# Row statistics of a layer norm: from one engine's statistics instruction to another's two accumulating passes

## The chip, the cores and the metric

The kernel runs on one core of a Trainium2 chip. The metric is the time on the device in microseconds (us), lower is better. Three runs of the kernel before took 1511.75, 1512.75 and 1513.91 us, so its median is 1512.75 us. The engines of a core: TensorE (PE in the profile; PEld are its weight loads), VectorE (DVE), ScalarE (ACT), GpSimd (POOL) and SyncE (SP), which here only issues DMAs. Each engine works through its own instructions in order and waits on semaphores for the others.

## The reference, cut to what matters

```python
def reference(x, adj, W_q, b_q, W_k, b_k, W_v, b_v):     # x: 4096 x 512, adj: 4096 x 4096 of 0 and 1
    m = mean(x, axis=-1); v = var(x, axis=-1)
    h = maximum((x - m) / sqrt(v + 1e-5), 0)             # layer norm of every row, then relu
    q, k, v = h @ W_q.T + b_q, h @ W_k.T + b_k, h @ W_v.T + b_v
    z = (q @ k.T) / sqrt(512) * adj
    z = where(z == 0, -10000.0, z)
    return x + relu(softmax(z, axis=1) @ v)
```

All inputs and the output are float32. The change concerns the first two lines alone.

## The kernel before, in words

The 4096 rows of x are cut into 32 tiles of 128 rows, and these into 8 quads of 4 tiles (QUAD, QUADS). The kernel has two parts.

The **opening** makes everything that the attention needs: the normalised rows h, their halves of 16 bits (a high and a low part, so that float16 products give nearly float32), V = h Wv, and G, the product of h with M = Wk Wq (project_g), in the form of seven operands of a Strassen-like product. It is a loop over k in 0 .. 40 that every engine walks in its own order: slot k = 4g + i, with i = 0 .. 3. In the text "slot i" means this i, and four slots make a period. In slot k:

- TensorE (lines 627 to 643): the first or third piece of the scores of one pair of tiles (`scores(begun, 0)` where i is odd, `scores(ended, 2)` where it is even), the V tile k (`project_v`, L475), the second or fourth piece of the scores, the transpose of h tile k + 4 (`transpose_h`, L457), and a part of G of the quad before (`project_g`, L489). Scores of pairs are made in the opening from slot 9 on. All products of the scores stand at L502.
- ScalarE (lines 836 to 875): `copy_m1` (L747) and `copy_m2` of the pair begun, or `copy_u4` and `copy_d` of the pair ended; `high_v(k)` (L705); `copy_u2`, `copy_m7` or `copy_c12`; `high_g` (L724) where i is 0 or 2; `high_h(k+4)` (L697); in slot i = 2 the root of the quad g + 2 (`square_root`, L681); `normalise(k+5)` (L688); and `copy_g` (L713). TensorE's next piece of the scores waits for the first copy of the pair (m1 or u4), because it accumulates into the same bank.
- VectorE (lines 1245 to 1303): `add_c2`, then in slot 3 `quad_rstd` (reciprocal of the root, one Newton step, and the shift, from L972 to L982), `combine_g`, `low_v` (L1009), `low_g` (L1029), `low_h` (L1003), `add_c11`, `weigh` (times the adjacency, L1101), `row_dot` (L990), `negate`, `see_min` (the running minimum, L1117), and in slot i = 1 the statistics of quad g + 2: four `row_stats` (L954), four `aggregate` (L960) and `quad_var` (L965 and L966).

The normalisation of a quad goes around the engines so: mean and variance on VectorE, `var_eps` (variance + epsilon), root on ScalarE, `quad_rstd` on VectorE, then `normalise` on ScalarE with scale and bias per row, one tile per slot. A quad of x is loaded by SP (`load_x`, L310) into one of two buffers, o_rows or p_buf, once the quad before in that buffer has been normalised: quads 0 and 1 at the start, quad 2 after the first, and `load_x(g + 3)` in period g.

The **main part** (L502 and L558 in turn) then goes over 8 blocks of 512 query rows with 16 pairs of key tiles each: scores, exponential, and the sum over V. It has no part in the change. Ahead of the opening's loop stands a start (lines 1197 to 1243 on VectorE, 821 to 834 on ScalarE) in which the quads 0 and 1 and the weights are prepared; there the statistics of quad 1 stand between `largest_m(1)` and `row_dot(2)`, and its aggregates after `low_h(3)`.

Of the kernel before, what the change touches and what calls it, by code (L numbers as in the profile page):

```python
# [13 lines left out]
P = 128  # L14
NODES = 4096
DIM = 512
# [32 lines left out]
def adj_preln_attention(nc, x, adj_t, wq, bq, wk, bk, wv_t, bv, out, g_dram, v_dram, h_dram):  # L49
# [15 lines left out]
    with ctx:  # L65
        def sb(name, shape, dt):
            return ctx.enter_context(nc.sbuf_tensor(name, shape, dt))
# [41 lines left out]
        b_cols = sb("b_cols", [P, 2, KC], F32)  # L109
        stats = sb("stats", [P, QUAD, 6], F32)  # L110
        mean_var = sb("mean_var", [P, QUAD, 2], F32)
        mean = sb("mean", [P, TILES], F32)
        var_eps = sb("var_eps", [P, TILES], F32)
        root = sb("root", [P, TILES], F32)
        rstd = sb("rstd", [P, TILES], F32)
# [79 lines left out]
        m_lo_ready = sem("m_lo_ready")  # L195
        stats_ready = sem("stats_ready")
        aggregated = sem("aggregated")
        var_ready = sem("var_ready")
        root_ready = sem("root_ready")
        newton_seq = sem("newton_seq")  # L200
# [476 lines left out]
        def _(act):  # L677
            def square_root(q):
                act.wait_ge(var_ready, q + 1)
                span = slice(q * QUAD, (q + 1) * QUAD)  # L680
                nc.scalar.activation(root[:, span], var_eps[:, span], ACT.Sqrt).then_inc(root_ready, 1)  # L681

            def normalise(t):
                act.wait_ge(rstd_ready, t // QUAD + 1)
                if t >= 2:
                    act.wait_ge(hT_ready, t - 1)
                    act.wait_ge(dots_done, t - 1)
                nc.scalar.activation(normal[t % 2], x_quad[t // QUAD % 2][:, t % QUAD, :], ACT.Relu,  # L688
                                     bias=shift[:, t:t + 1], scale=rstd[:, t:t + 1]).then_inc(normed, 1)
# [131 lines left out]
            square_root(0)  # L821
            normalise(0)
            normalise(1)
            act.wait_ge(wv_loaded, 16)
            for k in range(KC):
                high_wv(k)
# [1 line left out]
            high_h(1)  # L828
            normalise(2)
            normalise(3)  # L830
            high_h(2)
            high_h(3)
            square_root(1)
# [2 lines left out]
            for k in range(PARTS):  # L836
                g, i = k // QUAD, k % QUAD
                begun, ended = opening_pair(k), opening_pair(k - 1)
                if begun >= 0:
                    copy_m1(begun)  # L840
                    copy_m2(begun)
                if ended >= 0:
                    copy_u4(ended)
                    copy_d(ended)
                if k == 1:
                    high_m(0)
                    high_m(1)
                if k == 2:
                    high_m(2)
                    high_m(3)  # L850
                if g < QUADS:
                    high_v(k)
                if begun >= 0:
                    copy_u2(begun)
                    copy_m7(begun)
                if ended >= 0:
                    copy_c12(ended)
                if i == 2 and 1 <= g <= QUADS:
                    high_g(g - 1, 0)
                if i == 0 and 2 <= g <= QUADS + 1:  # L860
                    high_g(g - 2, 1)
                if g + 1 < QUADS:
                    high_h(k + QUAD)
                if k in (5, 6):
                    high_t(0, 2 * (k - 5))
                    high_t(0, 2 * (k - 5) + 1)
                if k in (36, 37):
                    high_t(1, 2 * (k - 36))
                    high_t(1, 2 * (k - 36) + 1)
                if i == 2 and g + 2 < QUADS:  # L870
                    square_root(g + 2)
                if k + QUAD + 1 < TILES:
                    normalise(k + QUAD + 1)
                if 1 <= g <= QUADS:
                    copy_g(g - 1, i)

            for n in range(-3, STEPS):
                s, j = n // PAIRS, n % PAIRS
# [47 lines left out]
        def _(dve):  # L926
# [19 lines left out]
                dve.wait_ge(scales_ready, k + 1)  # L946

            def row_stats(t):
                q = t // QUAD
                if t % QUAD == 0:  # L950
                    dve.wait_ge(x_loaded[q % 2], 16 * (q // 2 + 1))
                    if q > 0:
                        dve.wait_ge(aggregated, QUAD * q)
                v.bn_stats(stats[:, t % QUAD, :], x_quad[q % 2][:, t % QUAD, :]).then_inc(stats_ready, 1)  # L954

            def aggregate(t):
                dve.wait_ge(stats_ready, t + 1)
                if t % QUAD == 0 and t > 0:
                    dve.wait_ge(var_ready, t // QUAD)
                v.bn_aggr(mean_var[:, t % QUAD, :], stats[:, t % QUAD, :]).then_inc(aggregated, 1)  # L960

            def quad_var(q):
                span = slice(q * QUAD, (q + 1) * QUAD)
                dve.wait_ge(aggregated, QUAD * q + QUAD)
                v.tensor_copy(mean[:, span], mean_var[:, :, 0])  # L965
                v.tensor_scalar(var_eps[:, span], mean_var[:, :, 1], EPS, None, ALU.add).then_inc(var_ready, 1)  # L966

            def quad_rstd(q):
                span = slice(q * QUAD, (q + 1) * QUAD)
                r = rstd[:, span]  # L970
                dve.wait_ge(root_ready, q + 1)
                v.reciprocal(r, root[:, span]).then_inc(newton_seq, 1)  # L972
                dve.wait_ge(newton_seq, 4 * q + 1)
                v.tensor_tensor(newton[:, :], r, r, ALU.mult).then_inc(newton_seq, 1)
                dve.wait_ge(newton_seq, 4 * q + 2)
                v.scalar_tensor_tensor(out=newton[:, :], in0=newton[:, :], scalar=-0.5, in1=var_eps[:, span],
                                       op0=ALU.mult, op1=ALU.mult).then_inc(newton_seq, 1)
                dve.wait_ge(newton_seq, 4 * q + 3)
                v.scalar_tensor_tensor(out=r, in0=newton[:, :], scalar=1.5, in1=r,
                                       op0=ALU.add, op1=ALU.mult).then_inc(newton_seq, 1)  # L980
                dve.wait_ge(newton_seq, 4 * q + 4)
                v.scalar_tensor_tensor(out=shift[:, span], in0=mean[:, span], scalar=-1.0, in1=r,  # L982
                                       op0=ALU.mult, op1=ALU.mult).then_inc(rstd_ready, 1)

            def row_dot(t):
                dve.wait_ge(normed, t + 1)
# [216 lines left out]
                row_stats(t)  # L1203
            for t in range(QUAD):
                aggregate(t)
            quad_var(0)
            dve.wait_ge(u_row_ready, 1)
            v.tensor_copy(u_row, u_row_bank).then_inc(u_row_copied, 1)
            quad_rstd(0)
# [18 lines left out]
            link(largest(mag[1][:, KC:KC + 1], u_cols[:, :]))  # L1228
            link(v.tensor_scalar(mag[1][:, KC:KC + 1], mag[1][:, KC:KC + 1], 1.0 / DIM, None, ALU.mult))
            largest_m(1)  # L1230
            for t in range(QUAD, 2 * QUAD):
                row_stats(t)
            row_dot(2)
            low_h(2)
            row_dot(3)
            low_h(3)
            for t in range(QUAD, 2 * QUAD):
                aggregate(t)
            quad_var(1)
            key_terms(0)  # L1240
            largest_m(2)
            quad_rstd(1)
            largest_m(3).then_inc(mag_ready, 1)

            for k in range(PARTS + 2):
# [47 lines left out]
                if k in (37, 38):  # L1293
                    low_t(1, 2 * (k - 37))
                    low_t(1, 2 * (k - 37) + 1)
                if i == 1 and g + 2 < QUADS:
                    for t in range(QUAD):
                        row_stats(QUAD * (g + 2) + t)
                    for t in range(QUAD):
                        aggregate(QUAD * (g + 2) + t)  # L1300
                    quad_var(g + 2)
                if i == 3 and g + 1 < QUADS:
                    key_terms(g + 1)
# [98 lines left out]
```

## Time and profile before

| | |
|---|---|
| median of 3 runs | 1512.75 us |
| the profiled execution's own time | 1509.94 us |
| its span, first to last instruction | 1508.2 us |
| mean granted TensorE clock | 0.998 |
| TensorE busy | 1478.0 us, 98% of the span |
| VectorE busy | 1272.7 us, 84% |
| ScalarE busy | 878.8 us, 58% |
| GpSimd busy | 1.7 us |
| DMA | 304.92 MB, mean 202 GB/s |

The opening lasts from about 37 to 305 us of the span. How to read the profile: "line engine operation out<-in" is a group of instructions, with starts and durations in us from the span's start. Behind one another, operations of an engine overlap a little, so the distance from start to start is shorter than the duration. In square brackets stands for how long the engine was idle before, and what released it. The granted clock is a share of TensorE's full 2.4 GHz.

### The profile page before, as it was taken

The numbers are of one execution on the slowest core, as the hardware profiler recorded it, in microseconds if no ns is written. First come the engines' busy times: TensorE is split into PE (matmuls) and PEld (weight loads), VectorE is DVE, ScalarE is ACT, GpSimd is POOL, SyncE is SP. The second block draws the span as 40 slices with busy tenths as digits, with TensorE's granted clock in tenths as the row PEclk, the third lists the DMA queues.
The fourth block names the chain that finished last, engine by engine and source line by source line (L and its number), as shares of the span: only waits on it lengthen the run. The fifth ranks groups of instructions, "written<-read, shape, count | busy, mean of one in ns | idle before, by whom it ended". The sixth has DMA issues, their size and how long they took to land.

```text
span 1508.2 us, 24869 instructions
## 1 busy us (share of the span) xinstructions
PE 1478.0 (98%) x9550; PEld 941.3 (62%) x9550; DVE 1272.7 (84%) x1570; ACT 878.8 (58%) x1402; POOL 1.7 (0%) x11
## 2 busy tenths in 40 slices
PE   8899999889999999999999999999999999999998
PEld 4456665566666666666666666666666666666544
DVE  6878887898898889798988898889978897988875
ACT  2566665575566556665656555655665566555542
POOL 0000000000000000000000000000000000000000
PEclk9999999999999999999999999999999999999999
DMA  5255544485555655566646665566556655655252
GB/s 202 98 183 203 201 161 161 159 300 205 222 207 194 249 211 220 210 225 229 222 194 238 238 231 196 207 236 238 209 212 223 226 210 209 217 212 191 86 168 84
DMA packets 75478, 304.92 MB, mean 202 GB/s; under 512 B 8416, under 2 KB 8416, under 8 KB 73568
## 3 DMA queue, kind: packets, MB, share of 16 engines
q1 hardware_dynamic: 75360, 303.33, 54.6%
q8 instruction: 76, 1.25, 0.3%
q14 instruction: 42, 0.34, 0.1%
HBM read 264.51 MB, written 38.80 MB: 201 GB/s over the span
## 4 chain that ended last, share of the span: by engine, by line
PE 92%; DVE 4%; issue 2%; ACT 1%; DMA 1%; SPq 0%; DVEq 0%; POOLq 0%; POOL 0%; ACTq 0%
PE o L558 44%; PE za L502 22%; PE zd L502 11%; PE zb L502 5%; PE o L475 5%; PE o L489 4%; DMA o_rows<-in_x 1%; PE o L457 1%; DVE stats L954 0%; PE za L586 0%; DVE run_min L1117 0%; ACT g_buf L724 0%; PE za L578 0%; PE za L570 0%; DVE o_rows L1172 0%
## 5 line engine op out<-in xcount | busy, mean ns | idle before, releaser
L558 PE MATMUL o<-v_buf,p_buf 128*128 128x512 f16 x3072 | 734.8, 379 | 3.3 <-issue 3.3
L558 PEld LDWEIGHTS o<-v_buf,p_buf 128*128 128x128 f16 x3072 | 300.5, 98 | 272.0 <-issue 3.5
L502 PE MATMUL za<-h_buf,g_buf 128*128 128x256 f16 x2976 | 405.8, 273 | 7.6 <-ACT mm_tmp L747 3.4
L502 PEld LDWEIGHTS za<-h_buf,g_buf 128*128 128x128 f16 x2976 | 289.6, 98 | 144.8 <-ACT mm_tmp L747 5.3
L502 PE MATMUL zd<-h_buf,g_buf 128*128 128x256 f16 x1488 | 203.0, 273 | 0.0
L1093 DVE TENSOR_TENSOR slots<-um_tmp,dm_tmp 128x512 f32<-128x512 f32 x128 | 88.4, 690 | 108.8 <-ACT dm_tmp L774 108.7
L1140 DVE TENSOR_TENSOR p_buf<-slots,p_buf 128x1024 f16<-128x1024 f32 x128 | 156.1, 1219 | 21.7 <-PE o L558 20.1
L786 ACT ACTIVATE slots<-slots,log_p 128x1024 f32<-128x1024 f32 x128 | 145.9, 1140 | 37.3 <-DVE slots L1133 37.3
L781 ACT ACTIVATE slots<-za,c_all,kappa 128x256 f32<-128x256 f32 x128 | 72.3, 565 | 145.5 <-PE za L502 144.7
L1105 DVE SCALAR_TENSOR_TENSOR slots<-slots 128x1024 f32<-128x1024 f32 x128 | 156.0, 1219 | 0.2
L1133 DVE TENSOR_TENSOR slots<-slots,floor_b 128x1024 f32<-128x1024 f32 x128 | 155.8, 1218 | 0.4 <-ACT floor_b L799 0.4
L502 PEld LDWEIGHTS zd<-h_buf,g_buf 128*128 128x128 f16 x1488 | 145.6, 98 | 16.9
L747 ACT ACTIVATE mm_tmp<-za,c_all,kappa 128x256 f32<-128x256 f32 x128 | 72.4, 566 | 139.8 <-PE za L502 135.8
L1151 DVE TENSOR_TENSOR acc<-acc,slots 128x1024 f32<-128x1024 f32 x112 | 136.5, 1219 | 0.5
L1117 DVE TENSOR_TENSOR run_min<-run_min,slots 128x1024 f32<-128x1024 f32 x112 | 136.4, 1218 | 0.0
L793 ACT CAST p_buf<-slots 128x1024 f16<-128x1024 f32 x128 | 132.9, 1038 | 3.7 <-PE o L558 3.2
L1101 DVE TENSOR_TENSOR slots<-slots,adj_own 128x1024 f32<-128x1024 f32 x91 | 111.4, 1224 | 15.0 <-ACT slots L781 7.7
L759 ACT ACTIVATE um_tmp<-za,c_all,kappa 128x256 f32<-128x256 f32 x128 | 72.4, 566 | 70.8 <-PE za L502 62.7
L502 PE MATMUL zb<-h_buf,g_buf 128*128 128x256 f16 x744 | 101.5, 273 | 0.0
L769 ACT ACTIVATE um_tmp<-za,c_all,kappa 128x256 f32<-128x256 f32 x128 | 72.4, 566 | 47.9 <-PE za L502 47.2
L502 PEld LDWEIGHTS zb<-h_buf,g_buf 128*128 128x128 f16 x744 | 72.8, 98 | 8.4
L475 PE MATMUL o<-slots,h_buf 128*128 128x512 f16 x288 | 68.6, 389 | 4.7 <-DVE v_buf L1009 4.7
(151 smaller groups left out, 1104.7 us busy)
## 6 DMA issues: line engine op xcount, KB each, us to landing
g_buf<-g_dram SPq DMA_DIRECT2D x112, 896.0 KB, 5.4
v_buf<-v_dram SPq DMA_DIRECT2D x128, 512.0 KB, 3.4
adj_own<-in_adj SPq DMA_DIRECT2D x91, 512.0 KB, 6.2
spare<-in_adj SPq DMA_DIRECT2D x37, 512.0 KB, 6.2
g_dram<-g_buf SPq DMA_DIRECT2D x12, 896.0 KB, 4.5
v_dram<-v_buf SPq DMA_DIRECT2D x16, 512.0 KB, 5.3
spare<-in_x SPq DMA_DIRECT2D x15, 512.0 KB, 8.7
h_buf<-h_dram SPq DMA_DIRECT2D x7, 1024.0 KB, 9.1
```

The lines of the kernel that those rows point to most:

```text
L475: mm = pe.matmul(v_bank(t)[:, :], h[:, a, k, span], wv_pair[:, b, k, :], start=(k == 0 and m == 0), stop=(k == KC - 1 and m == 2))
L502: mm = pe.matmul(bank[:, 0:QH], g_of(i)[:, a, op, j, :], right[b][j], start=(fresh and j == 0 and m == 0), stop=(j == 1 and m == 2), skip_ ...
L558: mm = pe.matmul(o_bank[t][:, :], a[:, kt, span], v_buf[:, n % V_BUFS, kt, b, :], start=(j == 0 and kt == 0 and m == 0), stop=(j == PAIRS ...
L786: nc.scalar.activation(slot(n), slot(n), ACT.Exp, bias=log_p[:, 0:1], scale=-UNIT).then_inc(p_ready, 1)
L793: nc.scalar.copy(p_hi[n % 3], slot(n)).then_inc(p_hi_ready, 1)
L1093: v.tensor_tensor(slot(i)[:, 1, :], um_tmp[:, :, :].rearrange("p a n -> p (a n)"), dm_tmp[:, :, :].rearrange("p a n -> p (a n)"), ALU.add) ...
L1101: v.tensor_tensor(slot(i), slot(i), adj_buf[adj_slot(i)], ALU.mult).then_inc(weighted, 1)
L1105: v.scalar_tensor_tensor(out=slot(i), in0=slot(i), scalar=0.0, in1=slot(i), op0=ALU.is_equal, op1=ALU.subtract).then_inc(negated, 1)
L1117: v.tensor_tensor(run_min[:, :, :], run_min[:, :, :], slot(i), ALU.min).then_inc(min_seen, 1)
L1133: v.tensor_tensor(slot(n), slot(n), floor_b[:, :].unsqueeze(1).to_broadcast([P, 2, QW]), ALU.subtract).then_inc(lowered, 1)
L1140: v.tensor_tensor(p_lo[n % 2], slot(n), p_hi[n % 3], ALU.subtract).then_inc(p_lo_ready, 1)
L1151: v.tensor_tensor(acc[:, :, :], acc[:, :, :], slot(n), ALU.add).then_inc(summed, 1)
```

## The change

For quad 0 nothing changes but the sign that is kept with the mean. From quad 1 on the four `bn_stats`, four `bn_aggr` and the copy of the mean on VectorE are gone. In their place ScalarE goes twice over every tile of x: `row_mean` computes -x/512 into a float16 tile that nobody reads and sums it along the row into `neg_mean`, and `row_squares` computes (x + neg_mean) squared into the same tile and sums it into `squares`. `quad_var` on VectorE becomes one small operation, squares/512 + epsilon. In the loop the four mean passes of quad g + 2 stand at the end of ScalarE's slot i = 0, its four passes of squares at the end of slot i = 1, and `quad_var` at the end of VectorE's slot i = 2. `square_root` stays in the middle of ScalarE's slot i = 2.

```diff
+        neg_mean = sb("neg_mean", [P, TILES], F32)
+        squares = sb("squares", [P, TILES], F32)
+        sum_waste = sb("sum_waste", [P, 2, DIM], F16)
...
+            def row_mean(t):
+                q = t // QUAD
+                if t % QUAD == 0:
+                    act.wait_ge(x_loaded[q % 2], 16 * (q // 2 + 1))
+                    if q >= 2:
+                        act.wait_ge(squares_ready, t - QUAD)
+                elif t % QUAD >= 2:
+                    act.wait_ge(means_ready, t - QUAD - 1)
+                nc.scalar.activation(sum_waste[:, t % 2, :], x_quad[q % 2][:, t % QUAD, :], ACT.Copy, scale=-1.0 / DIM,
+                                     accum_out=neg_mean[:, t:t + 1]).then_inc(means_ready, 1)
+
+            def row_squares(t):
+                act.wait_ge(means_ready, t // QUAD * QUAD)
+                if t % QUAD >= 2:
+                    act.wait_ge(squares_ready, t - QUAD - 1)
+                nc.scalar.activation(sum_waste[:, t % 2, :], x_quad[t // QUAD % 2][:, t % QUAD, :], ACT.Square,
+                                     bias=neg_mean[:, t:t + 1], accum_out=squares[:, t:t + 1]
+                                     ).then_inc(squares_ready, 1)
...
             square_root(0)
             normalise(0)
             normalise(1)
+            for t in range(QUAD, 2 * QUAD):
+                row_mean(t)
             act.wait_ge(wv_loaded, 16)
...
             normalise(2)
             normalise(3)
+            for t in range(QUAD, 2 * QUAD):
+                row_squares(t)
             high_h(2)
...
                 if 1 <= g <= QUADS:
                     copy_g(g - 1, i)
+                if g + 2 < QUADS:
+                    for t in range(QUAD):
+                        if i == 0:
+                            row_mean(QUAD * (g + 2) + t)
+                        if i == 1:
+                            row_squares(QUAD * (g + 2) + t)
...
             def quad_var(q):
                 span = slice(q * QUAD, (q + 1) * QUAD)
-                dve.wait_ge(aggregated, QUAD * q + QUAD)
-                v.tensor_copy(mean[:, span], mean_var[:, :, 0])
-                v.tensor_scalar(var_eps[:, span], mean_var[:, :, 1], EPS, None, ALU.add).then_inc(var_ready, 1)
+                dve.wait_ge(squares_ready, QUAD * (q - 1) + QUAD)
+                v.tensor_scalar(var_eps[:, span], squares[:, span], 1.0 / DIM, EPS, ALU.mult, ALU.add
+                                ).then_inc(var_ready, 1)
...
-                v.scalar_tensor_tensor(out=shift[:, span], in0=mean[:, span], scalar=-1.0, in1=r,
-                                       op0=ALU.mult, op1=ALU.mult).then_inc(rstd_ready, 1)
+                v.tensor_tensor(shift[:, span], neg_mean[:, span], r, ALU.mult).then_inc(rstd_ready, 1)
...
             largest_m(1)
-            for t in range(QUAD, 2 * QUAD):
-                row_stats(t)
             row_dot(2)
             low_h(2)
             row_dot(3)
             low_h(3)
-            for t in range(QUAD, 2 * QUAD):
-                aggregate(t)
-            quad_var(1)
             key_terms(0)
             largest_m(2)
+            quad_var(1)
             quad_rstd(1)
             largest_m(3).then_inc(mag_ready, 1)
...
-                if i == 1 and g + 2 < QUADS:
-                    for t in range(QUAD):
-                        row_stats(QUAD * (g + 2) + t)
-                    for t in range(QUAD):
-                        aggregate(QUAD * (g + 2) + t)
+                if i == 2 and g + 2 < QUADS:
                     quad_var(g + 2)
```

## Rows read from the trace of the kernel before

**Rows 1.** Page, parts 1 and 4: busy us by engine; shares of the ending chain
```profile
PE 1478.0 (98%) x9550; PEld 941.3 (62%) x9550; DVE 1272.7 (84%) x1570; ACT 878.8 (58%) x1402; POOL 1.7 (0%) x11
...
PE 92%; DVE 4%; issue 2%; ACT 1%; DMA 1%; SPq 0%; DVEq 0%; POOLq 0%; POOL 0%; ACTq 0%
```

**Rows 2.** Stretches, us: busy and (count) by engine, granted clock, DMA share, GB/s
```profile
160.00:180.00 20.00, 20.00 (x124) 12.13 (x123) 17.27 (x40) 13.50 (x24) 0.00 (x0) 1.00 0.52 189
280.00:300.00 20.00, 13.86 (x99) 9.08 (x97) 17.45 (x23) 12.69 (x23) 0.00 (x0) 1.00 0.28 106
```

**Rows 3.** Timeline, ScalarE, 152 to 186 us: start, duration, line, [idle before <-releaser]
```profile
162.97 0.94 ACT L724 CAST g_buf<-slots 128x896 f16<-128x896 f32 x1 [0.91 <-DVE slots L1022]
...
164.66 0.58 ACT L697 CAST h_buf<-o 128x512 f16<-128x512 f32 x1
165.14 0.20 ACT L681 ACTIVATE root<-var_eps 128x4 f32<-128x4 f32 x1
165.24 0.80 ACT L688 ACTIVATE acc<-p_buf,shift,rstd 128x512 f32<-128x512 f32 x1
166.13 0.69 ACT L713 ACTIVATE slots<-o,u_cols 128x512 f32<-128x512 f32 x1
167.07 0.56 ACT L747 ACTIVATE mm_tmp<-za,c_all,kappa 128x256 f32<-128x256 f32 x1 [0.24 <-DVE slots L1085]
...
180.93 0.69 ACT L713 ACTIVATE slots<-o,u_cols 128x512 f32<-128x512 f32 x1 [0.18 <-DVE spare L1029]
181.89 0.56 ACT L747 ACTIVATE mm_tmp<-za,c_all,kappa 128x256 f32<-128x256 f32 x1 [0.27 <-DVE slots L1085]
```

**Rows 4.** Timeline, TensorE, 152 to 186 us
```profile
156.75 0.82 PE L502 MATMUL za<-h_buf,g_buf 128*128 128x256 f16 x6
...
164.33 0.82 PE L502 MATMUL za<-h_buf,g_buf 128*128 128x256 f16 x6
...
168.23 0.82 PE L502 MATMUL za<-h_buf,g_buf 128*128 128x256 f16 x6
...
184.05 0.82 PE L502 MATMUL za<-h_buf,g_buf 128*128 128x256 f16 x6
```

**Rows 5.** Timeline, VectorE, 152 to 186 us
```profile
158.46 2.47 DVE L954 BATCH_NORM_STATS2 stats<-o_rows 128x6 f32<-128x512 f32 x4
160.85 0.36 DVE L960 BATCH_NORM_AGGREGATE mean_var<-stats 128x2 f32<-128x6 f32 x4
...
165.96 0.68 DVE L1003 TENSOR_TENSOR h_buf<-o,h_buf 128x512 f16<-128x512 f32 x1
...
167.50 1.22 DVE L1117 TENSOR_TENSOR run_min<-run_min,slots 128x1024 f32<-128x1024 f32 x1
```

**Rows 6.** Timeline, all engines, 0 to 45 us
```profile
0.72 1.28 ACT L681 ACT_TABLE_LOAD   x1 [0.72 <-PEq L1389]
...
22.54 2.56 ACT L813 ACTIVATE slots<-slots,up 128x512 f16<-128x512 f32 x4 [3.00 <-DVE up L945]
...
23.64 0.08 DVE L990 DVE_READ_ACCUMULATOR half_min<-acc,floor_b 128x1 f32 x1
...
36.61 0.81 ACT L688 ACTIVATE acc<-p_buf,shift,rstd 128x512 f32<-128x512 f32 x1 [1.39 <-DVE shift L982]
```

**Rows 7.** Timeline, all engines, 45 to 95 us
```profile
51.67 5.28 PE L475 MATMUL o<-slots,h_buf 128*128 128x512 f16 x12 [3.08 <-DVE v_buf L1009]
...
76.28 0.66 PE L457 MATMUL o<-ident,acc 128*128 128x128 f32 x4 [0.70 <-ACT acc L688]
...
77.51 0.17 DVE L972 RECIPROCAL rstd<-root 128x4 f32<-128x4 f32 x1
```

**Rows 8.** Stretches of 2 us, TensorE alone: busy, granted clock
```profile
52.00:54.00 2.00, 2.00 (x6) 0.50 0.85 344
...
56.00:58.00 2.00, 2.00 (x11) 0.78 0.39 154
```

**Rows 9.** DMA issues, 0 to 100 us: KB each, median us to landing
```profile
p_buf<-in_x SPq DMA_DIRECT2D x2, 1024.0 KB, 9.8
```

More of the change, by code:

```diff
@@ L111, in adj_preln_attention @@
         mean_var = sb("mean_var", [P, QUAD, 2], F32)
-        mean = sb("mean", [P, TILES], F32)
+        neg_mean = sb("neg_mean", [P, TILES], F32)
+        squares = sb("squares", [P, TILES], F32)
+        sum_waste = sb("sum_waste", [P, 2, DIM], F16)
         var_eps = sb("var_eps", [P, TILES], F32)
@@ L197, in adj_preln_attention @@
         aggregated = sem("aggregated")
+        means_ready = sem("means_ready")
+        squares_ready = sem("squares_ready")
         var_ready = sem("var_ready")
@@ L948, in row_stats, with first_var @@
             def row_stats(t):
[L949 to L954, printed above, removed]
+                if t == 0:
+                    dve.wait_ge(x_loaded[0], 16)
+                v.bn_stats(stats[:, t, :], x_quad[0][:, t, :]).then_inc(stats_ready, 1)
             def aggregate(t):
                 dve.wait_ge(stats_ready, t + 1)
-                if t % QUAD == 0 and t > 0:
-                    dve.wait_ge(var_ready, t // QUAD)
-                v.bn_aggr(mean_var[:, t % QUAD, :], stats[:, t % QUAD, :]).then_inc(aggregated, 1)
+                v.bn_aggr(mean_var[:, t, :], stats[:, t, :]).then_inc(aggregated, 1)
+            def first_var():
+                dve.wait_ge(aggregated, QUAD)
+                v.tensor_scalar(neg_mean[:, 0:QUAD], mean_var[:, :, 0], -1.0, None, ALU.mult)
+                v.tensor_scalar(var_eps[:, 0:QUAD], mean_var[:, :, 1], EPS, None, ALU.add).then_inc(var_ready, 1)
             def quad_var(q):
                 span = slice(q * QUAD, (q + 1) * QUAD)
-                dve.wait_ge(aggregated, QUAD * q + QUAD)
-                v.tensor_copy(mean[:, span], mean_var[:, :, 0])
-                v.tensor_scalar(var_eps[:, span], mean_var[:, :, 1], EPS, None, ALU.add).then_inc(var_ready, 1)
+                dve.wait_ge(squares_ready, QUAD * (q - 1) + QUAD)
+                v.tensor_scalar(var_eps[:, span], squares[:, span], 1.0 / DIM, EPS, ALU.mult, ALU.add
+                                ).then_inc(var_ready, 1)
             def quad_rstd(q):
@@ L1205, in _ @@
                 aggregate(t)
-            quad_var(0)
+            first_var()
             dve.wait_ge(u_row_ready, 1)
```

## The prediction

> **What bounds the kernel now.** I read the page first: the busy shares and the shares of the chain that ended last [rows 1]. TensorE is busy for 98% of the span and makes 92% of the chain, so a microsecond counts only if TensorE waits for it. The change touches nothing after the opening (the 41 slots in which h, V and G are made), so next comes the table of stretches [rows 2]. From 160 to 180 us TensorE is busy for 20.00 of 20 us, VectorE for 17.27 and ScalarE for 13.50: all that the change can do to VectorE there is worth nothing, and all that makes ScalarE late for TensorE costs its full length. The reader is to see that ScalarE has 6.5 us free in 20, but in pieces between TensorE's results, not at its own choice.
>
> Third comes the timeline of each engine over one period of four slots, here those of g = 4 [rows 3 to 5]. Slot i = 2 starts on TensorE at 156.75, slot 3 at 164.33. In each slot TensorE's first two products and a V tile take 3.90 us (164.33 to 168.23), and then come products that need ScalarE's copy of the first one; in the next period's slot 1 that point is 184.05, so two slots are 15.8 us and a period 31.6 [rows 4]. ScalarE gives the first copy of slot 3 at 167.07 and of slot 1 at 181.89: 0.6 us of spare time in the one, 1.6 us in the other [rows 3, 4]. That is the room in which the change must fit. Fourth, the start of the kernel [rows 6, 7] and the granted clock there [rows 8]: until about 76 us TensorE waits for both of the other engines.
>
> **The change part by part.** *Removed from VectorE*, in slot 1: four statistics in 2.47 us, four aggregates in 0.36 and the copy of the mean, some 2.9 us in a period of 31.6 [rows 5]. One small tensor_scalar stays. Nothing in the steady part waits for this but the next combination of G: ScalarE's high half of G at 162.97 had been idle 0.91 us for it [rows 3]. So the removal brings 0.9 us of earlier high_g, and no TensorE time by itself. The four table entries turned from a fused multiply to a product, and the sign of the mean, change no count of instructions: nothing, hidden in VectorE's gaps.
>
> *Added to ScalarE*: eight passes over 128x512 in each period, four after copy_g of slot 0, four after copy_g of slot 1. The nearest row in form is the high half of Wv: SBUF f32 to f16, one pointer operand, four in 2.56 us, so 0.62 us each behind one another [rows 6]. An operation without a pointer, from PSUM, gives way after 0.48 us (164.66 to 165.14) [rows 3]; I take 0.52 for the mean pass. No row shows what reading ScalarE's accumulator costs. Bounds: nothing (VectorE's own such record is 0.08 us long and overlaps its neighbour [rows 6]) and 0.20 us, ScalarE's shortest operation (the root) in full; a gain is excluded, since work is only added. The root gives way to the next after 0.10 us [rows 3] and is the nearest thing, a tiny operation behind a long one on the same engine, so I take 0.10. A mean pass is then 0.62 us and a pass of squares 0.72; four are 2.5 us (2.1 to 3.3) and 2.9 us (2.5 to 3.7).
>
> The Trainium skill, "ScalarE: Activation LUTs", section "What ACT_TABLE_LOAD costs", has 186 ns + 0.833 ns per element, 93 ns for each pointer and 93 ns of overlap, and no price for the accumulator: 0.52 and 0.61 us a pass, bursts of 2.1 and 2.4 us. By that alone the sum below would come to about 8 us, not 11.6.
>
> *Term 1, slot 1.* copy_g at 180.93 gives way at about 181.5 [rows 3]. The means end at 184.0, the first copy of slot 1 (before at 181.89) at 184.6, and TensorE wants it at 184.05 [rows 3, 4]: 0.6 us of stall (0.2 to 1.4).
>
> *Term 2, slot 2.* copy_g comes 0.2 us after the slot's start, the squares run from +0.8 to +3.7, the copy that TensorE needs at +3.9 ends at +4.3: 0.4 us (0 to 1.2).
>
> *Term 3, the wait that is new.* The root stays where it was in ScalarE's order, in the middle of slot 2 (165.14), ahead of a normalise (165.24), copy_g (166.13) and slot 3's first copy (167.07) [rows 3]. What it waits for is now quad_var at the end of VectorE's slot 2, behind low_v, both low_g, low_h (165.96), the row dot and the running minimum, which begins at 167.50 and takes 1.14 us to the next [rows 5]: the slot ends at 168.64, which is +11.9. High_v is 0.5 us late through term 2, high_g no longer waits 0.9, so the slot ends at about +11.5, the root runs at +11.7, the normalise at +11.8, copy_g from +12.5, the first copy from +13.1 to +13.7. TensorE wants it at +11.5, plus the 0.4 of term 2. Stall: 1.75 us, and it hardly depends on the price of a pass. Behind the waiting root stand the normalise, copy_g and that copy, and TensorE, with its products of slot 3, waits for the last.
>
> These repeat in g = 3, 4 and 5: 3 x 2.75 = 8.25 us. In g = 2 there is no running minimum yet (1.14 us less in term 3) and ScalarE has no earlier pair to copy in slot 0, so term 1 is about nil: 0 + 0.4 + 0.6 = 1.0 us. From g = 6 on there are no more statistics.
>
> *Term 4, the start.* The means of tiles 4 to 7 fit in ScalarE's 3 us of waiting ahead of 22.54 [rows 6]. Their squares delay two copies of h, but VectorE is free of the statistics, so the first normalise of the second quad (36.61, where ScalarE had waited 1.39 us for VectorE [rows 6]) comes some 1.7 us earlier. That lead is lost at k = 2, where high_m now stands behind the squares and the root behind quad_var; the V tile that starts at 51.67 [rows 7] starts about 0.4 us later by my walk through the queues. At k = 6 term 3 is back: in the kernel before VectorE ended slot 2 at 77.51, where quad_rstd starts [rows 7]. Quad_var now stands there: root at 77.6, normalise to 78.5, and the transpose that started at 76.28 [rows 7] starts at 78.6: +2.3 us, and TensorE is saturated from 85 us on and never gets it back. Taken: 2.3 us (1 to 5, as the bursts at k = 4 and 5 vary by 0.8 each and both sit ahead of low_v).
>
> *Moved or hidden at no cost*: load_x waits for the same normalise, which is 3.5 us later in a period, and the mean pass wants its rows a slot sooner. It has about 12 us left (from 169.5 to 181.5), and a load into the same buffer landed in 9.8 us, the first ones behind the weights among them [rows 9]; SP's queue is passed by nothing new, the load keeps its place in it. POOL is untouched but for the second reduction, which comes 1.7 us earlier. With that cover gone, each late load would cost its own lateness.
>
> **Sum**: 8.25 + 1.0 + 2.3 = +11.6 us. The profiled execution took 1509.94 us (span 1508.2 and 1.7 around it), so 1521.5; the median of the runs shown lies 2.8 us above that execution, so 1524.4, given as 1524. With the low prices: 3 x 1.95 + 0.6 + 1 = 7.5 us, 1520; with the high ones 3 x 4.25 + 2.5 + 5 = 20 us, 1533.
>
> **Rivals.**
> *A gain by the clock.* The V tile at 51.67 took 5.28 us, twice what it needs, because the granted clock stood at 0.50 (1.2 of 2.4 GHz) from 52 us on, after TensorE had idled 3.08 us for VectorE's low_v, and was back between 56 and 58 us [rows 7, 8]. If VectorE's relief brings that tile forward by more than about 1.5 us, the clock stays up: about 2.5 us for the tile (half of 5.28) and 1.7 us of lead make -4.2 us, 1508.5. It needs low_v of tile 3 before 50 us, and the steady stalls to be nil. For it: VectorE was the last releaser there. Against: by the walk the seventh transpose waits for root and quad_var till about 51. Chance 0.05.
> *The stalls are given back.* TensorE idles 6.1 us between 280 and 300 us [rows 2]. If what binds there were VectorE's backlog, lateness of TensorE before would be hidden and the time would stay at 1512 to 1515. Against: VectorE is 2.7 us idle in 20 while TensorE is saturated [rows 2], so it carries no backlog; the waits at 280 us are latencies that start from TensorE's own results and shift with them. Chance 0.08.
> *Table loads.* One load of 1.28 us at 0.72 [rows 6] serves Sqrt, Relu, Copy and Identity all through the opening. If Square is not among its functions, each period has two more loads, one before the squares and one before the root, both on the path above: 2.6 us for each of the four late periods and some 2.6 at the start, 13 us on top: 1537. Chance 0.04. The Trainium skill, "ScalarE: Activation LUTs", "Table sets: the hidden batching unit", counts cheap functions as filler of every set, and does not list square for the set of sqrt; it puts a switch at about 2.66 us with its drain, which would make it 1551.
> *The forecast*, slower by terms 1 to 4: 0.83, with its prices between both ends.
>
> **How the numbers follow.** 1524 is the likeliest case's sum. The range 1516 to 1532 holds the forecast but for its last tips; the rivals on either side are left out, 0.17, with a little of the tips. A measurement of this kernel can tell about 0.2% (3 us) from no change. Faster by more: 0.05. Within: 0.08. Slower: 0.87.
>
> **What would show it.** In the changed kernel: ScalarE's root idle ahead of it for VectorE's var_eps about 3.5 us once in each period from 90 to 210 us; TensorE idle before L502 of slot 3 about 1.7 us, released by ScalarE's first copy, and before that of slots 1 and 2 by 0.6 and 0.4; a transpose near 78.6 in place of 76.28; VectorE less busy by some 20 us and ScalarE more by 18 to 25. I am wrong if TensorE stays saturated from 90 to 210 us, if a pass takes over 0.9 us, or if the root doesn't wait.

## The result and the profile after

The changed kernel took 1522.39 us (median of 4 runs, 1521.71 to 1523.51), the kernel before 1513.33 us beside it (4 runs): a ratio of 1.0061 with a 95% interval of 1.0047 to 1.0074, so 9 us slower, between 7 and 11. The forecast was 11.6 us slower, 1524. The profiled execution of the changed kernel took 1522.1 us with a span of 1519.9: 11.7 us over the span before, because the execution profiled before lies 3 us under its median.

The page of the changed kernel, the parts of [rows 1], and its stretch from 160 to 180 us, as in [rows 2]:

```profile
PE 1481.6 (97%) x9550; PEld 941.0 (62%) x9550; DVE 1254.9 (83%) x1507; ACT 911.0 (60%) x1514; POOL 1.7 (0%) x11
...
PE 88%; DVE 5%; ACT 5%; issue 2%; DMA 0%; DVEq 0%; SPq 0%; ACTq 0%
```

```profile
160.00:180.00 20.00, 18.44 (x118) 11.32 (x117) 13.26 (x26) 14.67 (x32) 0.00 (x0) 1.00 0.35 111
```

VectorE lost 17.8 us of busy time (I had written some 20) and ScalarE gained 32.2 (I had written 18 to 25, against my own prices: 28 passes of each kind at 0.62 and 0.72 are 37.5). TensorE has the same work, but in a stretch in which it was busy for 20.00 of 20 us it now is for 18.44, and 5% of the chain that ended last is ScalarE's.

The timeline of ScalarE in the changed kernel over the slots of [rows 3], i = 1 to 3 of g = 4, which now lie some 7 to 8 us later:

```profile
156.74 0.62 ACT L695 ACTIVATE sum_waste<-o_rows 128x512 f16<-128x512 f32 x1
157.25 0.19 ACT L695 ACTIVATION_READ_ACCUMULATOR sum_waste<-o_rows 128x1 f32 x1
157.35 0.61 ACT L695 ACTIVATE sum_waste<-o_rows 128x512 f16<-128x512 f32 x1
...
159.19 0.54 ACT L770 ACTIVATE mm_tmp<-za,c_all,kappa 128x256 f32<-128x256 f32 x1
...
164.34 0.69 ACT L736 ACTIVATE slots<-o,u_cols 128x512 f32<-128x512 f32 x1 [1.29 <-PE o L493]
164.92 0.71 ACT L702 ACTIVATE sum_waste<-o_rows,neg_mean 128x512 f16<-128x512 f32 x1
...
167.74 0.55 ACT L792 ACTIVATE um_tmp<-za,c_all,kappa 128x256 f32<-128x256 f32 x1
...
171.35 0.58 ACT L720 CAST h_buf<-o 128x512 f16<-128x512 f32 x1
175.53 0.21 ACT L685 ACTIVATE root<-var_eps 128x4 f32<-128x4 f32 x1 [3.60 <-DVE var_eps L998]
175.64 0.80 ACT L711 ACTIVATE acc<-p_buf,shift,rstd 128x512 f32<-128x512 f32 x1
176.34 0.67 ACT L736 ACTIVATE slots<-o,u_cols 128x512 f32<-128x512 f32 x1
176.91 0.55 ACT L770 ACTIVATE mm_tmp<-za,c_all,kappa 128x256 f32<-128x256 f32 x1
```

Each pass is two instructions: the activation and a read of the accumulator of 0.19 us, which starts before the activation has ended. Four means stand between copy_g and the first copy of slot 1 (159.19), four passes of squares between copy_g (164.34) and the first copy of slot 2 (167.74). The third stall is the one to look at: after high_h at 171.35 ScalarE does nothing for 3.60 us, and the root that ends this idle time is released by VectorE's var_eps. In [rows 3] the root had no bracket at all, so it waited for nothing that the timeline shows. TensorE over the same stretch, the products of [rows 4]:

```profile
159.79 0.83 PE L506 MATMUL za<-h_buf,g_buf 128*128 128x256 f16 x6 [0.36 <-ACT mm_tmp L770]
...
168.35 0.83 PE L506 MATMUL za<-h_buf,g_buf 128*128 128x256 f16 x6
...
172.04 0.82 PE L506 MATMUL za<-h_buf,g_buf 128*128 128x256 f16 x6
...
177.52 0.83 PE L506 MATMUL za<-h_buf,g_buf 128*128 128x256 f16 x6 [1.42 <-ACT mm_tmp L770]
```

Stalls of 0.36 us ahead of slot 1's products and 1.42 us ahead of slot 3's, both released by the copy L770 (the L747 of before). The one ahead of 168.35 is too short for a bracket. VectorE shows why var_eps is late:

```profile
171.64 1.08 DVE L1061 TENSOR_TENSOR spare<-slots,spare 128x896 f16<-128x896 f32 x1
172.65 0.68 DVE L1035 TENSOR_TENSOR h_buf<-o,h_buf 128x512 f16<-128x512 f32 x1
...
174.19 1.22 DVE L1149 TENSOR_TENSOR run_min<-run_min,slots 128x1024 f32<-128x1024 f32 x1
175.33 0.16 DVE L998 TENSOR_SCALAR var_eps<-squares 128x4 f32<-128x4 f32 x1
```

It is the last operation of VectorE's slot 2, behind low_g, low_h, the row dot and the running minimum, as in [rows 5]. Summed over 80 to 240 us, in the table of waits of the changed kernel:

```profile
ACT root L685 <- DVE var_eps L998: 13.2, 4, 3.6
PEld za L506 <- ACT mm_tmp L770: 9.0, 7, 1.9
```

Four waits, one in each of g = 2 to 5. And the start, TensorE's timeline with the places of [rows 7] (the brackets are idle time before), and the granted clock there:

```profile
51.70 1.11 PE L461 MATMUL o<-ident,acc 128*128 128x128 f32 x4 [4.41 <-ACT acc L711]
52.99 3.80 PE L479 MATMUL o<-slots,h_buf 128*128 128x512 f16 x12 [0.17 <-DVE v_buf L1041]
...
77.67 0.66 PE L461 MATMUL o<-ident,acc 128*128 128x128 f32 x4 [2.84 <-ACT acc L711]
78.34 4.44 PE L493 MATMUL o<-h_buf,slots 128*128 128x512 f16 x12
```

```profile
80.00:82.00 2.00, 2.00 (x6) 0.50 1.04 407
```

The transpose of 76.28 stands at 77.67, after 2.84 us of idle time in place of 0.70, and the twelve products behind it took 4.44 us because the clock stood at 0.50 (1.2 GHz).

### The profile page after: what moved, and what is told of

The parts are those of the page before. It is cut to its first block, busy times and chain, and to the rows that moved or that the text cites. A ratio compares the mean times of both kernels' runs of the same rounds, so it can differ in the third digit from the quotient of the medians.

```text
span 1519.9 us, 24924 instructions
## 1 busy us (share of the span) xinstructions
PE 1481.6 (97%) x9550; PEld 941.0 (62%) x9550; DVE 1254.9 (83%) x1507; ACT 911.0 (60%) x1514; POOL 1.7 (0%) x11
## 4 chain that ended last, share of the span: by engine, by line
PE 88%; DVE 5%; ACT 5%; issue 2%; DMA 0%; DVEq 0%; SPq 0%; ACTq 0%
PE o L562 43%; PE za L506 21%; PE zd L506 11%; PE zb L506 5%; PE o L493 3%; PE o L479 2%; DVE g_buf L1061 1%; ACT sum_waste L695 1%; ACT sum_waste L702 1%; ACT g_buf L747 1%; PE o L461 1%; PE za L596 0%; DVE run_min L1149 0%; PE za L590 0%; ACT slots L736 0%
## 5 line engine op out<-in xcount | busy, mean ns | idle before, releaser
L562 PE MATMUL o<-v_buf,p_buf 128*128 128x512 f16 x3072 | 734.9, 379 | 3.3 <-issue 3.3
L562 PEld LDWEIGHTS o<-v_buf,p_buf 128*128 128x128 f16 x3072 | 300.6, 98 | 271.8 <-issue 3.5
L506 PE MATMUL za<-h_buf,g_buf 128*128 128x256 f16 x2976 | 405.8, 273 | 11.4 <-ACT mm_tmp L770 6.7
L809 ACT ACTIVATE slots<-slots,log_p 128x1024 f32<-128x1024 f32 x128 | 145.9, 1140 | 37.3 <-DVE slots L1165 37.3
L770 ACT ACTIVATE mm_tmp<-za,c_all,kappa 128x256 f32<-128x256 f32 x128 | 72.2, 564 | 137.8 <-PE za L506 135.9
L479 PE MATMUL o<-slots,h_buf 128*128 128x512 f16 x288 | 67.1, 383 | 1.2 <-DVE v_buf L1041 1.2
```

The costliest lines, as they stand in the source:

```text
L479: mm = pe.matmul(v_bank(t)[:, :], h[:, a, k, span], wv_pair[:, b, k, :], start=(k == 0 and m == 0), stop=(k == KC - 1 and m == 2))
L506: mm = pe.matmul(bank[:, 0:QH], g_of(i)[:, a, op, j, :], right[b][j], start=(fresh and j == 0 and m == 0), stop=(j == 1 and m == 2), skip_ ...
L562: mm = pe.matmul(o_bank[t][:, :], a[:, kt, span], v_buf[:, n % V_BUFS, kt, b, :], start=(j == 0 and kt == 0 and m == 0), stop=(j == PAIRS ...
L809: nc.scalar.activation(slot(n), slot(n), ACT.Exp, bias=log_p[:, 0:1], scale=-UNIT).then_inc(p_ready, 1)
```

## The experiments

All are compared by two distances in TensorE's timeline: **start**, from the first to the ninth V tile, and **later**, from the ninth to the 31st. (L475 before, 32.45, 79.53 and 252.29 us; L479 after, 34.16, 82.61 and 264.03.) Each distance is read from one profiled execution; the measured ratio compares the medians of all runs.

| kernel | start, us | later, us | sum against before | ratio measured, 95% |
|---|---|---|---|---|
| before | 47.08 | 172.76 | 0 | |
| changed | 48.45 | 181.42 | +10.0 | 1.0047 to 1.0074 |
| 1 quad_var first | 44.74 | 176.49 | +1.4 | 1.0006 to 1.003 |
| 2 root late | 46.42 | 176.80 | +3.4 | 1.0013 to 1.003 |
| 3 late quad_var alone | 49.67 | 182.00 | +11.8 | 1.0081 to 1.0118 |
| 4 passes alone | 49.74 | 176.20 | +6.1 | 1.003 to 1.0061 |
| 5 passes spread | 44.86 | 173.70 | -1.3 | 0.998 to 0.9999 |
| 6 quads 1 to 3 only | 44.40 | 172.76 | -2.7 | 0.9969 to 0.9986 |
| 7 passes, no accumulator | 47.94 | 173.74 | +1.8 | one run |
| 8 quad 1 only | 43.66 | 172.76 | -3.4 | 0.9973 to 0.9991 |
| 9 quads 1 and 2 | 44.99 | 172.76 | -2.1 | 0.9991 to 1.0009 |

The distances leave out both ends of an execution, and these differ too. The first V tile starts at 32.45 us in before, 32.49 in 2, and 33.85 to 35.49 in all the others. From the 31st V tile to the end of the span it is 1255.9 us in before, the changed kernel and 2, 1257.1 to 1257.9 in most others, 1259.4 in 3 and 1259.6 in 9; from 300 to 350 us the granted clock was 1.00 in before, 0.90 in 3 and 0.93 in 9. In 3 and 9 the measured interval lies above the sum (12 to 18 us against 11.8, and -1.4 to +1.4 against -2.1); the late end of their profiled executions is enough for that, but whether it is as late in their other runs isn't shown.

My theory after the result: most of the loss is the root's wait for quad_var, the rest is the two bursts. The rival: ScalarE's added 5.3 us a period are too much, and the root only stands behind them.

**1. quad_var ahead of low_v.**

```diff
+                if i == 2 and g + 2 < QUADS:
+                    quad_var(g + 2)
                 if g < QUADS:
                     low_v(k)
...
-                if i == 2 and g + 2 < QUADS:
-                    quad_var(g + 2)
```

> The changed kernel with quad_var moved on VectorE from the end of slot 2 to ahead of low_v of the same slot; ScalarE's passes stay. Theory (the wait of the root for quad_var is most of the loss, the bursts are the rest): the stalls of 1.42 us ahead of slot 3 vanish in g = 3, 4, 5, the stalls of 0.3 to 0.5 us ahead of slots 1 and 2 stay, the root no longer waits 3.6 us, the transpose at 77.7 us comes 2 us earlier; time 7 to 10 us under the changed kernel, so 0 to 3 us above the kernel before. Rival (the bursts on ScalarE are the loss, the root only stands behind them): under 3 us gained.

Measured: 1515.49 us against 1513.0 for the kernel before, so the loss went from 9 to between 1 and 4.5 us. Slot 1, and the slot 3 that had stalled by 1.42 us, on TensorE in this kernel:

```profile
154.37 0.83 PE L506 MATMUL za<-h_buf,g_buf 128*128 128x256 f16 x6 [0.36 <-ACT mm_tmp L770]
...
170.52 0.82 PE L506 MATMUL za<-h_buf,g_buf 128*128 128x256 f16 x6
```

The product at 170.52 has no bracket: the third stall is gone and the first is unchanged. On ScalarE the root runs without a wait:

```profile
166.41 0.21 ACT L685 ACTIVATE root<-var_eps 128x4 f32<-128x4 f32 x1
166.51 0.81 ACT L711 ACTIVATE acc<-p_buf,shift,rstd 128x512 f32<-128x512 f32 x1
```

"Later" fell by 4.93 us (expected 3 x 1.58 and about 0.45), "start" by 3.71. One line moved on another engine takes back most of the change's cost, with every pass in its place. The rival falls.

**2. The root behind slot 3's first copies.**

```diff
-                if i == 2 and g + 2 < QUADS:
-                    square_root(g + 2)
...
+                if i == 3 and g + 2 < QUADS:
+                    square_root(g + 2)
                 if k == 1:
                     high_m(0)
```

> The changed kernel with the root moved on ScalarE from the middle of slot 2 to slot 3, behind its first two copies; quad_var stays at the end of VectorE's slot 2. Theory: the same wait is taken off by the other side, so the stall ahead of slot 3 goes from 1.42 us to about nil in g = 3, 4, 5; 5 to 9 us under the changed kernel. The price may be VectorE, which then waits for the root at the head of its slot 3, ahead of low_v: under 1 us a period if anything. Rival (bursts): under 3 us gained.

Measured: 1516.78 us against 1513.0 (2 to 4.5 us by the interval). "Later" is 176.80, 0.3 us from the first experiment's: the wait can be undone from either side, by an earlier producer or by a consumer that stands behind what TensorE needs.

**3. The wait without the passes.** The kernel before, with

```diff
                         aggregate(QUAD * (g + 2) + t)
+                if i == 2 and g + 2 < QUADS:
                     quad_var(g + 2)
```

> The kernel before, statistics on VectorE, with one edit: quad_var at the end of VectorE's slot 2, as in the change. Theory: the wait alone costs 1.5 to 2.7 us in each of g = 3, 4, 5 (here high_g is not early, so up to a microsecond more than in the changed kernel), about 1 in g = 2 and 2 to 4 at the start: 8 to 14 us over the kernel before. Rival (bursts): within 3 us of the kernel before.

Measured: 1528.27 us against 1513.0, 15 us and more than the changed kernel lost (12 to 18 by the interval, where I had expected 8 to 14). No pass stands on ScalarE here. TensorE, ahead of slot 3 of g = 4:

```profile
179.35 0.83 PE L502 MATMUL za<-h_buf,g_buf 128*128 128x256 f16 x6 [2.21 <-ACT mm_tmp L747]
```

2.21 us in place of 1.42. The root runs at 177.36, which is +11.9 from the slot's start in place of +11.4, since high_g is not early when VectorE keeps the statistics; the other 0.3 us are the stall of slot 2, which TensorE doesn't have here. Of the three full periods the second and the third are each 2.38 us longer than before. The first (g = 3), with the same 2.21 us gap, is 4.05 us longer, and there the granted clock fell:

```profile
142.00:144.00 2.00, 0.34 (x3) 1.00 0.42 15
144.00:146.00 2.00, 2.00 (x13) 0.56 0.70 252
146.00:148.00 2.00, 2.00 (x9) 0.59 0.66 257
148.00:150.00 2.00, 2.00 (x12) 1.00 0.02 4
```

**4. The passes without the wait.** The kernel before with row_mean and row_squares at the change's places on ScalarE. Their sums are computed and nobody uses them; VectorE's statistics are the ones in use.

```diff
...
+                if g + 2 < QUADS:
+                    for t in range(QUAD):
+                        if i == 0:
+                            row_mean(QUAD * (g + 2) + t)
+                        if i == 1:
+                            row_squares(QUAD * (g + 2) + t)
```

> The kernel before, its statistics on VectorE in use, with ScalarE's eight passes for each quad from 1 on added where the change has them, their sums unused. Theory: only the bursts, 0.53 + 0.33 us in each of g = 3, 4, 5, about 1 in g = 2, and perhaps 1 to 3 at the start: 3 to 6 us over the kernel before. Rival (bursts are the loss): 8 us or more.

Measured: 1520.23 us against 1513.0, 7 us more (4.5 to 9 by the interval; I had expected 3 to 6). "Later" is 3.44 us longer: the bursts, as expected. The rest is at the start, where ScalarE is late and VectorE is not relieved: I had 1 to 3 us for it, and 2.7 came. Both parts together (3 and 4) would be 18 us by the distances; the change costs 10. Of the 8 between them 1.7 are the clock of one period of 3, and 0.8 in each full period is the shorter third stall. The rest, 3.9 us, lies in the start, where the relief of VectorE is the likely cause; no run takes it apart.

**5. The same passes, spread.** The first experiment, and in g = 2 to 5 the passes where ScalarE waits for TensorE anyway.

```diff
+            plan = {(0, 0): ("m0", "m1", "m2"), (1, 0): ("m3", "s0"), (1, 1): ("s1",), (2, 0): ("s2", "s3")}
...
+                stat_passes(g, i, 0)
                 if g < QUADS:
                     high_v(k)
...
+                stat_passes(g, i, 1)
                 if 1 <= g <= QUADS:
                     copy_g(g - 1, i)
```

> The changed kernel with quad_var ahead of low_v as in the first experiment, and in g = 2 to 5 the eight passes laid in ScalarE's idle places instead of two bursts: three means ahead of high_v in slot 0, the fourth and the first squares there in slot 1, the second squares ahead of copy_g of slot 1, the last two ahead of high_v in slot 2 (a second pair of waste tiles lets the two kinds alternate). Theory (the place of the passes costs, not their sum): the stalls ahead of slots 1 and 2 vanish, the V tiles from the 9th on keep the distance of the kernel before, 3.5 us under the first experiment, so 0 to 3 us under the kernel before. Rival (ScalarE's added 5.3 us a period are too much wherever they stand): no better than the first experiment, 2 to 4 us over the kernel before.

Measured: 1512.68 us against 1514.03, 0 to 3 us under the kernel before. From the tenth V tile (88.31) to the 31st (254.05) it takes 165.74 us, the same to the digit as before (86.55 to 252.29): the eight passes cost TensorE nothing there. What is left is one stall in g = 2, where the means ahead of high_v delay high_g:

```profile
82.54 0.63 ACT L693 ACTIVATE sum_waste<-o_rows 128x512 f16<-128x512 f32 x1 [1.30 <-DMA o_rows<-in_x]
...
86.99 0.83 PE L506 MATMUL za<-h_buf,g_buf 128*128 128x256 f16 x6 [0.86 <-DVE g_buf L1068]
```

It isn't the length of the passes that does it: the first mean waits 1.30 us for its rows of x to be loaded, and the next copy, high_v, starts at 84.40. Without that wait the three means would have ended at 83.10 (an estimate), about when this V tile is ready. It is the only pass of this kernel that waits for a load.

**6. Only the early quads on ScalarE.** The first experiment with quads 4 to 7 back on VectorE (`first_var` is the small operation behind the aggregates):

```diff
-                if g + 2 < QUADS:
+                if g < 2:
                     for t in range(QUAD):
...
+                if i == 2 and g < 2:
+                    quad_var(g + 2)
...
+                if i == 1 and 2 <= g < QUADS - 2:
+                    for t in range(QUAD):
+                        row_stats(QUAD * (g + 2) + t)
+                    for t in range(QUAD):
+                        aggregate(QUAD * (g + 2) + t)
+                    first_var(g + 2)
```

> The first experiment's kernel with ScalarE's passes for quads 1 to 3 alone; quads 4 to 7 get their statistics on VectorE in slot 1, as in the kernel before. Theory: from the 9th V tile on no stall at all, and what the relief of VectorE brings at the start (the 9th V tile 0.6 us earlier than before, and 2.3 when the start's own 1.7 us are taken off) is kept: 0 to 3 us under the kernel before. Rival (the start gains nothing that lasts): the kernel before, within 1 us either way.

Measured: 1510.56 us against 1514.03, 2 to 4.7 us under the kernel before and some 12 under the changed one: a version that beats both. "Later" is that of before; by the distances the gain of 2.7 us is all at the start.

**7. The price of the accumulator.** The fourth experiment without `accum_out`, and with a constant bias for the squares.

> The fourth experiment's kernel with its eight unused passes written without the accumulator output (and a constant bias for the squares). It measures what reading the accumulator costs. Theory: no accumulator reads in the trace, a mean pass 0.52 us start to start in place of 0.61, a pass of squares 0.61 to 0.62 in place of 0.71, so the burst is 0.37 us shorter and the stalls of a period go from 0.86 to about 0.2 us; some 3 us under the fourth experiment. Rival (the read overlaps and is free): the same distances and stalls as in the fourth.

One run of 1515.0 us. ScalarE's timeline, four merged passes of each kind and what follows them:

```profile
153.34 2.18 ACT L696 ACTIVATE sum_waste<-o_rows 128x512 f16<-128x512 f32 x4
155.43 0.55 ACT L771 ACTIVATE mm_tmp<-za,c_all,kappa 128x256 f32<-128x256 f32 x1
...
161.16 2.55 ACT L704 ACTIVATE sum_waste<-o_rows,log_p 128x512 f16<-128x512 f32 x4
163.62 0.55 ACT L793 ACTIVATE um_tmp<-za,c_all,kappa 128x256 f32<-128x256 f32 x1
```

2.09 us for four means and 2.46 for four passes of squares, so 0.52 and 0.61 each, against 0.61 and 0.71 with the read. "Later" is 0.98 us over the kernel before in place of 3.44. A full period loses 0.16 us in place of 0.85, so the eight reads of a period, 0.09 us each or 0.7 together, were most of the two stalls.

**8 and 9. Which early quad?** The sixth experiment with quad 1, or quads 1 and 2, on ScalarE.

```diff
-                if g < 2:
+                if g + 2 <= 1:
```

The ninth has 2 for the 1, and VectorE's statistics in the loop begin with the next quad.

> As the sixth experiment, but only quad 1 has its statistics on ScalarE; quads 2 to 7 are on VectorE as in the kernel before. Which quad's relief brings the gain of the sixth? If it is quad 1 (the first normalise of quad 1 was 2.5 us earlier against the start), the second V tile starts 2.5 us earlier against the first and most of that lasts: 2 to 3 us under the kernel before. If it is quad 2 (VectorE's four statistics at 44 us stand ahead of low_m and of the root that the eighth transpose needs), the lead is lost again by the fifth V tile: within 1 us of the kernel before.

> As the sixth experiment, with quads 1 and 2 on ScalarE. If quad 3 adds nothing: as the sixth, 2 to 4 us under the kernel before, and the eighth V tile waits for VectorE about 1.6 us again, as in the kernel before, in place of 1.06. If quad 3 matters: 1 to 2 us over the sixth.

Measured: 1511.43 us (quad 1 alone, 0.9973 to 0.9991) and 1513.45 us (both, 0.9991 to 1.0009), against 1512.74. Quad 1 alone has the shortest start of all, and its lead lasts here, which in the changed kernel is 2.5 us at the second V tile and 0.4 at the fifth. The first V tile is followed by the second after 3.02 us (5.52 before), and the fifth comes 16.68 us after the first (19.22 before), although it waits for VectorE as long as in [rows 7]. It also takes 4.44 us in place of 5.28:

```profile
50.53 4.44 PE L479 MATMUL o<-slots,h_buf 128*128 128x512 f16 x12 [3.08 <-DVE v_buf L1048]
```

Quad 2 on ScalarE gives part of that back: in the ninth experiment the fifth V tile comes 18.16 us after the first, and the transpose at 44.11 us waits for a normalise that stands behind quad 2's means:

```profile
44.11 0.65 PE L461 MATMUL o<-ident,acc 128*128 128x128 f32 x4 [1.09 <-ACT acc L711]
```

With quad 3 added (the sixth) the start was 0.6 us shorter again, and the wait of the eighth V tile 1.06 in place of 1.57. The ninth's time, though, is neither of the two that I had expected: it is that of the kernel before, while its distances are 2.1 us shorter. Between 6 and 8 the measurement can't choose.

## Why the prediction was right

**The bound.** TensorE was the bound of the opening and ScalarE's idle pieces the room, as read from [rows 2 to 4]. VectorE's relief brought the steady part nothing: "later" in 6, 8 and 9, with statistics on VectorE, is exactly that of the kernel before.

**The price of a pass.** I took 0.62 and 0.72 us, measured are 0.61 and 0.71. The root in [rows 3] was a good stand-in for the read of the accumulator: a record of 0.19 us of which 0.09 count. The seventh experiment gives 0.52 and 0.61 without it, so these 0.09 us are most of the first two stalls. By the formula of the Trainium skill, "ScalarE: Activation LUTs", section "What ACT_TABLE_LOAD costs", a pass was estimated at 0.52 and 0.61 us. The seventh experiment's trace agrees with it; the section has no term for the accumulator.

**Terms 1 to 3.** From the starts of the V tiles, a full period lost 0.53 (forecast 0.6), 0.33 (0.4) and 1.58 us (1.75): 2.44 in place of 2.75, three times over. (The high end's 4.25 a period should be 4.35 by the terms' own upper bounds, 1.4 + 1.2 + 1.75; the 1533 stays.) The third was a little too large because high_v came 0.3 us late (168.55, +4.4 from the slot's start at 164.13) and not 0.5, so the root ran at +11.4 and not +11.7. In g = 2 it was 1.33 us from the ninth to the 13th tile where I had 1.0: I had the first term there at nil, as ScalarE has no earlier pair to copy, but copy_g is held by low_g and the means start as late as in the other periods; that cost 0.65. Together 8.66 us against 9.25. That the third term hardly depends on the price of a pass is shown by the third experiment, which has it without any pass.

**Term 4, the start.** It was +1.4 us in the profile, not +2.3, and for reasons of which I had half. Right was the place at k = 6, where root and transpose wait for quad_var: 2.84 us of idle time in place of 0.70, so 2.1 us, nearly all of the 2.3. Right was also that quad 1's lead goes at k = 2, but not its size: the second V tile came 2.5 us earlier against the first, not 1.7, and the fifth was still 0.4 us earlier, where I had 0.4 later. With quad_var early (experiment 1) 1.0 us of the lead is left there, and without quad 2's passes (experiment 8) all of its 2.5, so the passes take more of it than the root's wait. The eighth waited 1.03 us for VectorE in place of 1.58. Not in my sum at all was the clock: it was back earlier in the fifth V tile (3.80 us in place of 5.28, a gain of 1.5) and fell a second time behind the longer idle time at k = 7 (4.44 us in place of 2.75, a loss of 1.7). That these two nearly cancel is luck.

**The rivals.** The gain by the clock needed the fifth V tile 1.5 us earlier; in the changed kernel it stood 1.3 us later by the span's time and 0.4 earlier against the first V tile, and the steady stalls were there. In the kernels of 6 and 8 the gain exists, but through quad 1's lead (1.0 and 2.5 us at the fifth V tile) more than the clock (0.8 us in that tile). An earlier tile alone doesn't keep the clock up: in experiment 1 the wait ahead of it was 1.32 us in place of 3.08, behind one of 2.60 ahead of the transpose, and it took 4.83 us. The stalls were not given back: the 31st V tile is 11.74 us later than before and the first product of L562 after the opening 11.76 us (340.31 against 328.55). There is no second table load: the groups of the root's line over the first 270 us of the changed kernel are

```profile
L685 ACT ACTIVATE root<-var_eps 128x4 f32<-128x4 f32 x8 | 1.6, 205 | 34.3 <-DVE var_eps L998 19.8 <-DVE var_eps L993 14.5
L685 ACT ACT_TABLE_LOAD x1 | 1.3, 1283 | 0.7 <-PEq L1413 0.7
```

one load at the start. ScalarE's only other load stands ahead of the first exponential (L809), so Square is served by the table that serves Sqrt. The section "Table sets: the hidden batching unit" of the same page of the Trainium skill counts cheap functions as filler of every set and names relu, copy, identity and abs. Square isn't among those that it names; here it ran under the set that was loaded for Sqrt.

**The time.** Of the 11.7 us between the two spans, 8.66 are terms 1 to 3, 1.4 the start, and 1.7 stand ahead of the first V tile; these are all there at 12.76 us, before ScalarE's first pass at 20.28, so they aren't the change's. By the medians the difference is 9.1 us, and the forecast of 11.6 lies a little outside its interval of 7 to 11: the steady terms were sized 0.6 us too high and the start 0.9. The other 0.9 us, between the 10.0 of the distances and the 9.1 of the medians, no run explains; it is less than the interval's half width.

## What to carry to other kernels

When a producer is moved to another engine, look at every instruction in the consumer's queue behind the one that now waits: here a root of 0.2 us waited 3.6 us for the end of another engine's slot, with the copies for the bounding engine behind it, and one line moved (quad_var ahead of low_v) undid 8.6 of the 10 us by the distances of the table. An engine that is 58% busy has room only in the pieces between its inputs, so lay added work into the places where it waits, one to three operations each, but not ahead of the load that it reads: over the four periods the same eight passes cost 3.7 us as two bursts (experiment 1) and 0.9 when spread (experiment 5), all of it in one period, where a pass waited for its rows. Relieve an engine where it is on the path: by the distances the statistics of quad 1 alone gave 3.4 us, those of all seven quads, at their best places, 1.3. The measured times don't tell these two apart.

## What the runs showed that I had not expected

The clock adds chance to a stall. In the third experiment a 2.21 us gap of TensorE came three times, and once the granted clock went to 0.59 and 0.56 in the stretches behind it and cost 1.67 us more (4.05 in place of 2.38). The same wait of 3.08 us ahead of the fifth V tile was followed by a tile of 5.28 us in the kernel before and of 4.44 us in the eighth experiment. In the changed kernel 2.84 us of idle time cost 1.69 us on top. And ahead of all of the change, the clock of the stretch from 5 to 10 us was 1.00 in one execution and 0.74 in the other, where the same eight first products took 3.67 and 5.17 us (before, then changed):

```profile
7.55 3.67 PE L602 MATMUL o<-slots,row_acc 128*128 128x512 f32 x8 [2.37 <-DMA slots<-in_L_gnn_W_k]
7.75 5.17 PE L606 MATMUL o<-slots,row_acc 128*128 128x512 f32 x8 [3.10 <-DMA slots<-in_L_gnn_W_k]
```

That is most of the 1.7 us by which the first V tiles differ. Of the eleven profiled executions only those of before and of experiment 2 have the 3.67; the others have 5.10 to 6.71, so the trace of before is one of the lucky ones, as its time of 1509.94 us under a median of 1513 says too. Runs of one kernel, the kernel before from 1509.9 to 1516.9 us, spread by more than several of the effects here. So the distances within a trace told causes apart better than single times did, and only the medians of many runs say what a version is worth: experiment 9 was 2 us shorter by its distances and no faster.
